# First attention: part of the softmax denominators summed on PE instead of POOL, and the max pass one step later

## What is computed

```
x = x_bld + attention(layernorm(x_bld))      x_bld: 2 x 1024 x 128, 16 heads of 64
q       = x Wq                               per head 64
latent  = x Wkv_down                         32 wide, shared by the heads
k, v    = latent Wk_up, latent Wv_up
attn    = softmax(mask(q k / sqrt(64)), over keys)
out     = (attn v) Wout
```

## Time and profile before

| | us |
|---|---|
| median of 3 runs (lowest, highest) | 2145.34 (2144.02, 2146.32) |
| span of the profiled execution, first to last instruction | 2143.9 |
| PE busy, share of the span | 1852.0, 86% |
| DVE busy | 1659.2, 77% |
| ACT busy | 1124.7, 52% |
| POOL busy | 1004.6, 47% |

### The profile page before, as it was taken

The page is one execution under the profiler, slowest core; times in us unless marked ns, Lnnn a source line. Parts: engine busy times, 40 slices in busy tenths (PEclk is TensorE's granted clock), DMA queues, the critical chain, the costliest instruction groups (busy, mean ns, idle before and its releaser), DMA issues.

```text
span 2143.9 us, 32414 instructions
## 1 busy us (share of the span) xinstructions
PE 1852.0 (86%) x12284; PEld 1195.9 (56%) x12284; DVE 1659.2 (77%) x2131; ACT 1124.7 (52%) x1868; POOL 1004.6 (47%) x386
## 2 busy tenths in 40 slices
PE   6989898876888986799999978898888777899998
PEld 4444454445444445576777745555555455677776
DVE  4666555539799997667778599999999999876666
ACT  2344544433534322255555557777677676655554
POOL 3367766732266751101000068888889889500000
PEclk9799999988899998799999998999999999999999
DMA  3111202000200001001000000000001000010000
GB/s 84 31 31 31 44 21 55 4 12 1 50 0 0 1 0 35 15 19 31 30 30 15 1 1 2 2 2 2 1 2 31 2 2 1 30 30 30 15 16 20
DMA packets 35680, 39.13 MB, mean 18 GB/s; under 512 B 5891, under 2 KB 22534, under 8 KB 35526
## 3 DMA queue, kind: packets, MB, share of 16 engines
q1 hardware_dynamic: 34998, 36.01, 6.7%
q10 hardware_dynamic: 528, 1.05, 0.2%
HBM read 21.05 MB, written 1.05 MB: 10 GB/s over the span
## 4 chain that ended last, share of the span: by engine, by line
PE 49%; issue 17%; DVE 17%; POOL 10%; ACT 4%; SPq 1%; DMA 1%; DVEq 0%; ACTq 0%; POOLq 0%; PEldq 0%
PE ps L46 9%; PE ps L48 8%; PE ps L47 8%; DVE negm L2641 6%; POOL AF L733 3%; PE ps L537 3%; PE ps L521 3%; PE ps L562 2%; PE ps L2553 2%; PE ps L2470 2%; POOL AF L1552 2%; POOL AR_plain L2446 1%; PE ps L2544 1%; POOL hc L1552 1%; PE ps L570 1%
## 5 line engine op out<-in xcount | busy, mean ns | idle before, releaser
L2641 DVE TENSOR_REDUCE negm<-ps 128x64 bf16<-128x1024 f32 x256 | 302.1, 1215 | 20.6 <-PE ps L2544 20.5
L733 POOL TENSOR_TENSOR AF<-AF 128x2048 f32<-128x2048 f32 (+3 forms) x73 | 234.2, 3208 | 154.6 <-ACT AF L673 148.5
L2446 POOL TENSOR_TENSOR AR_plain<-AF 128x2048 f32<-128x2048 f32 x64 | 261.8, 4095 | 31.7 <-ACT AF L2597 31.4
L46 PE MATMUL ps<-XH,AR 128*128 128x512 f32 x616 | 255.2, 414 | 13.7 <-DVE XL L251 4.0
L2605 ACT ACTIVATE AF<-ps 128x1024 f32<-128x1024 f32 x192 | 196.3, 1023 | 134.4 <-PE ps L2553 132.9
L47 PE MATMUL ps<-XL,AR 128*128 128x512 f32 x616 | 245.7, 399 | 0.0
L48 PE MATMUL ps<-XH,AR 128*128 128x512 f32 x616 | 245.5, 399 | 0.0
L673 ACT ACTIVATE AF<-ps 128x512 f32<-128x512 f32 (+1 forms) x304 | 155.5, 576 | 148.2 <-PE ps L524 86.9
L2553 PE MATMUL ps<-negm,ident_bf 128*128 128x512 bf16 x512 | 162.0, 400 | 80.0 <-DVE negm L2641 79.6
L2648 DVE TENSOR_REDUCE AF<-AF 128x128 f32<-128x2048 f32 x96 | 218.6, 2277 | 0.0
L285 POOL TENSOR_SCALAR var_eps<-mv 128x8 f32<-128x8 f32 x10 | 4.2, 421 | 369.6 <-DVE mv L262 369.5
(11 more groups left out here) (336 smaller groups left out, 4371.6 us busy)
## 6 DMA issues: line engine op xcount, KB each, us to landing
AR<-AR SPq DMA_DIRECT2D x96, 128.0 KB, 2.4
AF<-in_L_ffn_Wg_dram SPq DMA_DIRECT2D x21, 256.0 KB, 2.8
AF<-in_L_ffn_Wu_dram SPq DMA_DIRECT2D x21, 256.0 KB, 3.1
AF<-in_L_ffn_Wd_dram SPq DMA_DIRECT2D x21, 256.0 KB, 3.9
AF<-AF SPq DMA_DIRECT2D x16, 64.0 KB, 2.4
AF<-AR_plain SPq DMA_DIRECT2D x16, 64.0 KB, 2.4
AF<-in_L_attn_a_Wq_dram SPq DMA_DIRECT2D x1, 512.0 KB, 4.1
AF<-in_L_attn_a_Wout_dram SPq DMA_DIRECT2D x1, 512.0 KB, 9.2
```

Source lines behind the costliest of these rows:

```text
L46: pe.matmul(out, ah, bh, start=start, stop=False)
L733: pool.tensor_tensor(zacc[u % 2][:, :, c0:512], zacc[u % 2][:, :, c0:512], pt[t % 4][:, :, 0:w], ALU.add).then_inc(s0_zp, 1)
L2446: pool.tensor_tensor(p6[m % 3].rearrange("p (j q i) -> p j q i", j=HJ, i=2), e6[m % 4].rearrange("p (j q i) -> p j q i", j=HJ, i=2), w6i[: ...
L2641: dve.tensor_reduce(negm6[:, j % 4, :], bank(2 * (j % 3), 2).rearrange("p (j q i) -> p q j i", j=HJ, i=2), mybir.AxisListType.XY, ALU.max, ...
```

## The change

- `late(t)` names the last three key blocks (n = 5, 6, 7) of the eight-block units, but for the last unit, which stays as it is. POOL no longer adds them.
- Item `z` of such a unit, after its four matmuls over `zacc`, goes on with twelve over the three buffers `pt`, into the same bank. It waits for the exponentials of the unit too.
- ACT, before it overwrites one of these buffers four steps later, waits until `z` is through on PE.
- The max pass of the next group is put one step later: its items stand in steps t0 + 3 to t0 + 13 in place of t0 + 2 to t0 + 12 (t0 is the step at which the group before begins). The last two, a `d` and the `n` of the c = 1 unit, so come into the step that has `z` of the c = 1 unit before them. The `q` items stay where they were.

```
 PE_SUMS = (NG0 - 1, 1)
+def late(t):
+    gg, c, n = STEPS[t]
+    return c == 1 and n >= 5 and (gg, c) != PE_SUMS
+def pooled(t):
+    return STEPS[t][2] > 0 and STEPS[t][:2] != PE_SUMS and not late(t)
...
-            ADDS_TO.append(ADDS_TO[-1] + (1 if STEPS[t][2] and STEPS[t][:2] != PE_SUMS else 0))
+            ADDS_TO.append(ADDS_TO[-1] + (1 if pooled(t) else 0))
...
-        plan(diagonal(1, 0) + [("n", 1, 0)] + full(1) + diagonal(1, 1) + [("n", 1, 1)], range(4, 13),
-             (5, 4, 4, 4, 4, 5, 6, 6, 2))
+        plan(diagonal(1, 0) + [("n", 1, 0)] + full(1) + diagonal(1, 1) + [("n", 1, 1)], range(4, 14),
+             (4, 4, 4, 4, 4, 5, 5, 5, 3, 2))
...
-                 range(t0 + 2, t0 + 13), (4, 5, 3, 3, 3, 3, 3, 4, 4, 5, 3))
+                 range(t0 + 3, t0 + 14), (4, 4, 3, 3, 3, 3, 4, 4, 5, 5, 2))
...
                     pe.wait_ge(s0_zp, ADDS_TO[LAST[u] + 1])
+                    last = [t for t in range(LAST[u] - 2, LAST[u] + 1) if late(t)]
+                    if last:
+                        pe.wait_ge(s0_e, SLOT_OF[LAST[u] + 1])
                     for h in range(4):
-                        ins = pe.matmul(o[LD * h:LD * h + LD, :], ones32, zacc[u % 2][:, h, :], start=True, stop=True)
+                        ins = pe.matmul(o[LD * h:LD * h + LD, :], ones32, zacc[u % 2][:, h, :], start=True,
+                                        stop=not last, skip_group_check=True)
+                    for t in last:
+                        c0, w = width(t)
+                        for h in range(4):
+                            ins = pe.matmul(o[LD * h:LD * h + LD, c0:512], ones32, pt[t % 4][:, h, 0:w], start=False,
+                                            stop=t == LAST[u], skip_group_check=True)
...
                         wait(act, s0_zp, ADDS_TO[max(0, t - 3)])
+                        if t >= 4 and late(t - 4):
+                            act.wait_ge(s0_a, AT[("z", 2 * STEPS[t - 4][0] + 1)] + 1)
...
-                if n and (gg, c) != PE_SUMS:
+                if pooled(t):
```

## The result

| | before | after |
|---|---|---|
| median of six runs each, us | 2145.74 | 2136.01 |
| lowest, highest | 2144.02, 2150.40 | 2128.56, 2139.39 |
| span of the profiled execution | 2143.9 | 2137.3 |

The ratio is 0.995, with an interval of 0.9935 to 0.9964: faster by 0.5%, which is more than a measurement of this kernel leaves open. The forecast was 2147.8 and "no change that counts". The time lies in the range of 2131 to 2159, on the other side of the kernel before. The profiled execution took 2139.04 us, 1.7 more than its span; it is the second slowest of the six.

What follows compares the result with a forecast made beforehand. PE bounds the kernel, with its idle time and low clock to win. Four boundaries at +0.8, two at +1.4 and -3.5 at the last give +2.5 on 2143.9, 2146.4; the median's 1.4 makes 2147.8 us, range 2131 to 2159.

Steps and rivals of the forecast that it cites:

- POOL's wait: PE's wait for POOL's additions before odd units' denominators; with its low clock 5.8 us at each of four boundaries, removed.
- the query DMAs' wait: PE's wait for DMAs spreading a group's queries, units 1 and 9; with low clock 5.2 us per boundary, removed.
- head groups of 48 to 49 us: Expected sign in the first attention: each head group takes 48 to 49 us instead of 47.2 to 47.7.
- The sums, 1.85 us: Twelve matmuls added on PE per odd unit, behind the denominators' old matmuls, at 1.85 us per unit.
- The new wait, 2.95: PE waits 2.95 us at item n behind the denominators for DVE's last maximum, in place of 3.15 for POOL.
- The four-block unit's n, +0.5: Item n of the four-block unit, now behind its denominators, waits 0.9 us against 0.41: +0.5 us per boundary.
- The last boundary: Behind unit 13, where no max pass follows: POOL's shorter chain brings the next denominators 3.5 us earlier.
- The clock: Half clock behind the new wait at item n, taken as 1.7 us at each of six boundaries.
- the clock stays up: Rival: the clock stays at 2.4 GHz behind the new wait, six times 1.7 us less: 2137.6, chance 0.22.
- A repair of POOL's wait alone: Removing only PE's wait for POOL would win next to nothing, since the DMA wait stands right behind it.
- The sums do not overlap across heads: Rival: each head takes the time of four in the twelve matmuls, 5.8 us more seven times; 2188 at most, chance 0.03.
- The wait for item n is hidden: Rival: ACT or DVE finish earlier, so PE's wait at item n goes six times: 25.6 us less, 2122, chance 0.08.

Runs made afterwards that it cites:

- Run 1: Changed kernel with the max pass back at its old steps, so only the sums move from POOL to PE: 2143.25 us, ratio 0.9995 against the kernel before.
- run 5: Changed kernel with the last d and n ahead of z behind eight-block units, and ACT's part of z behind all four exponentials: 2120.22 us, ratio 0.989.
- run 6: Changed kernel with ACT taking z's logarithm and exponential ahead of the two exponentials that wait for z: 2118.83 us, ratio 0.989.
- run 3: Changed kernel with the max pass in ten steps of four items, so that n comes before z: 2152.29 us, ratio 1.0026.
- run 7: The changed kernel once more, unedited, for a second profile: 2136.74 us, ratio 0.9964 against the kernel before.
- run 8: Changed kernel with d, n, z order behind eight-block units and z of four-block units behind the last d of its step: 2116.88 us, ratio 0.9865.

## Why the prediction was right and wrong

**The mechanism stood.** Item `n` waits for DVE seven times (forecast about 3 us, measured 2.67); POOL's wait and the query DMAs' wait went; twelve matmuls per unit came; half clock stands behind six of the seven waits; the last denominators follow at 15.7 us (about 15 forecast). One sign failed: head groups of 48 to 49 us. They are 47.8, 45.7, 47.3, 48.9 and 45.3 us long (the one that holds output projections as well is left out), where before they were 47.2, 47.7, 47.7, 47.2 and 45.5.

**The steps that failed are sizes in the sum**: what is added on PE (1.85 us for the sums), the new waits, and the half clock behind unit 14's wait, which the sum put at nothing. The span was forecast 2.5 us longer and came out 6.6 shorter, a miss of 9.1. Up to the last matmuls of the output projection it is larger: 9.3 us shorter in place of 2.5 longer, 11.8 us. The 2.7 us by which the rest of the program is longer hide a part.

- *The sums, 1.85 us.* Measured 1.30: where one group of four heads follows another they overlap by some 0.2 us, and the prediction took off 0.07 in all. The trace before had it: the denominators last 1.07 us and the values start 0.88 after them. Six times 0.55 = 3.3 us.
- *The new wait, 2.95.* Measured 2.67: six times 0.28 = 1.7 us. The walk along ACT and DVE was right (4.6 us for the forecast 4.8).
- *The four-block unit's n, +0.5.* It waits 0.62 instead of 0.41 in five groups, and in the sixth (unit 8) its wait of 0.94 is gone: +0.1 in all in place of +3.0. 2.9 us.
- *The last boundary.* Its 3.5 us came (3.2). Left out was that half clock had followed the 3.42 us wait of unit 14. It went with the wait: from unit 14's denominators to the last matmuls of the output projection it is 28.3 us in place of 30.8, 2.5 us.

**The clock**, the term that I could not read, was right in this profile: 1.7 us at each of six boundaries, 10.2 us. Its price can be read from the lengths between the denominators of eight-block units: 45.7 us from unit 3 to 5, with no half clock; 47.3 from 5 to 7, with 3.4 us of it; 48.8 from 9 to 11, with 6.8 us; and 48.5 from 1 to 3, where PE is busy in only 5.96 of the 6.8. With three stretches of 3.4 us and these two of 6.8 that is 3 x 1.6 + 3.1 + 2.8 = 10.7. It is luck in part: one boundary has nothing and two have nearly twice the forecast.

Together these make 9.6 us of the 11.8. Of the rest, the start of unit 1's denominators is 1.9 us earlier (121.53 for 123.46), where nothing had been costed: the old wait of `n` there was 0.96 us, not 0.38, and it went with a `d` and the `n` themselves to behind them. The remainder stays open, and so does the 1.1 us of the longer rest of the program that its first row does not hold.

**From the profile to the median** another 2.7 us are missing. The forecast put the median 1.4 us above its sum, as before; after's profiled execution is a slow one of its kind, and the median lies 1.3 us below its span.

**The range and the chances.** The first three mis-sized terms lie on one side, and they add up to 1.3 us per boundary outside the last. The prediction says itself that 1 us in each boundary is 6 us, and yet gave the faster side only a little of the forecast's 0.45: where a term comes back at each of six boundaries, its error does too. The rival whose time came out, *the clock stays up* (2137.6), did not happen by its mechanism: the half-clock stretches are there.

**A repair of POOL's wait alone** was said to win next to nothing. Run 1's ratio is 0.9995, and the DMA wait stands behind as said; that it stands at its full 3.5 us is not so (1.2 to 2.4 us), since the sums on PE (1.30 us) and a wait for ACT of 0.65 us cover a part of it.

**The rivals.** *The sums do not overlap across heads* fell: L602's rows hold 1.48 us for twelve matmuls. The rule of the Trainium skill, "FP8 and Floating Point Precision", section TensorE Precision Notes, that FP32 takes four passes, gave an estimate of 5.1 us per unit with one head after another; the trace doesn't go by it for four heads beside each other. *The wait for item n is hidden* did not happen, and run 5 shows what it brings: 16.5 us against the change in the same job (2120.22 for 2136.74), where 25.6 had been worked out. That its time is close to the forecast 2122 is luck, since the sum it was taken from was too high.

## What to carry to other kernels

When a wait is to be removed, look for the next one behind it first: what is won is the difference between the two (run 1). Then look at where the time went in the profiles of each half before you call both necessary. When an item is moved behind another on several in-order engines, walk the whole chain on each of them, and let the engine that feeds the others do its short operations first: one move on ACT (run 6) was worth more than the whole change. A wait that comes back at every boundary may cost more by the clock behind it than by the idleness: here 11.8 us against 8.0 on balance.

## What the runs showed of the hardware

- Groups of four FP32 matmuls in different columns of PE overlap not only among themselves but with the next group: 512, 384, 256 and 128 wide in a row took 2.18 us up to the next group's start.
- The clock fell to 1.2 GHz behind waits as short as 1.17 us (run 1 at unit 1, with one of 0.64 us just before it), 1.27 us (run 3) and 1.47 us (run 6, twice in seven), and stayed at 2.4 GHz behind one of 2.67 us (174.0 to 180.8, clock 1.00). Behind equal waits the low stretch was 3.4 or 6.8 us. What decides it is left open.
- A half-clock stretch of 3.4 us at a boundary cost 1.6 us, one of 6.8 us with PE busy throughout 3.1 us.
- The spread of the runs does not follow from these stretches alone: 14 us in ten runs of the changed kernel (run 7), 10 us in six of run 5 and 11 us in four of run 6, whose profiles have hardly any between units 1 and 14, and 2.3 us in four of run 8. Where it comes from is open.
